# VectorE builds eight selection matrices with two wide operations in a graph network kernel

## The reference, cut to what matters

```python
h = maximum(layernorm(x), 0)
for W, root, b in three_layers:                       # indices 0, 1, 2
    out = h @ root + b
    for r in range(8):
        mask = edge_type == r
        agg = segment_sum(where(mask, (h @ W[r])[src], 0), dst)
        cnt = segment_sum(mask, dst)
        out = out + agg / maximum(cnt, 1)
    h = relu(out)
x = x + h
h = maximum(layernorm(x), 0)
a = h + segment_sum(h[src], dst)
x = x + batchnorm(relu(a @ W1 + b1) @ W2 + b2)
```

## Time and profile before

| what | us |
|---|---|
| median of three runs | 1883.6 (1880.57 to 1884.61) |
| profiled execution, whole time | 1885.77 |
| its span, first to last instruction | 1883.8 |
| TensorE, VectorE, ScalarE, GpSimd busy | 1277.2, 888.7, 645.7, 1612.1 |

### The profile page before, as it was taken

How to read it: one execution, slowest core, us unless ns; L and a number is a source line. 1 busy time by engine, 2 the same in 40 slices (tenths; PEclk the granted TensorE clock), 3 DMA queues, 4 the chain that set the end, 5 groups by cost and what they waited for, 6 DMA issues and landing times.

```text
span 1883.8 us, 18726 instructions
## 1 busy us (share of the span) xinstructions
PE 1277.2 (68%) x4614; PEld 863.5 (46%) x4614; DVE 888.7 (47%) x3270; ACT 645.7 (34%) x1146; POOL 1612.1 (86%) x2502
## 2 busy tenths in 40 slices
PE   7888665657476776666667666675566666667787
PEld 3564444434344554444444344454444444444554
DVE  5784754545442366757676666652222222122213
ACT  5404000000000376867677766732011011112123
POOL 5888888888888888888888888878888888888881
PEclk9987655555555655657565656575567675757678
DMA  7823332323232311213121312231111111111111
GB/s 240 288 81 90 102 116 71 112 72 103 80 90 62 97 46 45 90 46 90 45 90 45 91 45 79 58 96 45 46 45 45 46 45 45 46 45 46 46 46 45
DMA packets 70010, 144.25 MB, mean 77 GB/s; under 512 B 23487, under 2 KB 37048, under 8 KB 69896
## 3 DMA queue, kind: packets, MB, share of 16 engines
q0 software_dynamic: 39840, 81.67, 17.3%
q1 hardware_dynamic: 29624, 60.67, 8.9%
q10 hardware_dynamic: 432, 0.64, 0.1%
HBM read 100.23 MB, written 42.67 MB: 76 GB/s over the span
## 4 chain that ended last, share of the span: by engine, by line
POOL 75%; issue 11%; PE 9%; DMA 4%; DVE 1%; ACT 1%; another core or an unknown queue 0%; POOLq 0%; DVEq 0%; SPq 0%; ACTq 0%
POOL rows L1249 53%; POOL slow L1234 19%; DMA rows<-h_table,idx 3%; PE ps_agg L562 2%; POOL early L1239 2%; PE ps_agg L617 1%; PE ps_a L580 1%; PE ps_h L531 1%; POOL rows L1270 1%; PE ps_agg L591 1%; PE ps_a L669 0%; PE ps_a L649 0%; PE ps_a L603 0%; PE ps_h L669 0%; ACT early L733 0%
## 5 line engine op out<-in xcount | busy, mean ns | idle before, releaser
L1249 POOL DMA_INDIRECT rows<-h_table,idx x1183 | 1127.4, 953 | 199.7 <-issue 190.2
L562 PE MATMUL ps_agg<-sel,rows 128*128 128x64 f32 (+16 forms) x2780 | 734.6, 381 | 452.2 <-DMA rows<-h_table,idx 445.3
L562 PEld LDWEIGHTS ps_agg<-sel,rows 128*128 128x128 f32 x2780 | 638.7, 290 | 725.3 <-DMA rows<-h_table,idx 539.3
L964 DVE TENSOR_SCALAR sel<-iota,early,norm 128x64 f32<-128x64 f32 x1186 | 436.8, 430 | 474.4 <-PE ps_agg L562 451.9
L1234 POOL MEMSET slow<- 128x264 f32 (+1 forms) x1248 | 424.1, 340 | 0.7
L1060 DVE TENSOR_TENSOR early<-ps_a,early 128x300 f32 x416 | 197.5, 475 | 207.9 <-PE ps_a L649 160.9
L846 ACT ACTIVATE scratch<-scratch,ones 128x300 bf16<-128x300 f32 x416 | 222.6, 535 | 119.6 <-PE ps_a L649 96.6
L649 PE MATMUL ps_a<-scratch 128*128 128x300 bf16 x416 | 168.3, 405 | 113.5 <-issue 67.7
L852 ACT ACTIVATE scratch<-iota,code_lo 128x300 f32<-128x300 f32 x416 | 226.5, 545 | 12.5
L531 PE MATMUL ps_h<-w_all,xT 128*128 128x512 f32 x300 | 214.1, 831 | 6.6 <-issue 4.9
L942 DVE TENSOR_SCALAR_CACHE_REDUCE agg_s<-scratch,key_f 128x256 bf16<-128x256 int16 x416 | 194.8, 476 | 7.0 <-DMA scratch<-key_rows 5.5
(11 more groups left out here) (158 smaller groups left out, 760.5 us busy)
## 6 DMA issues: line engine op xcount, KB each, us to landing
h_table<-stage SPq DMA_DIRECT2D x65, 512.0 KB
rows<-h_table,idx POOLq DMA_INDIRECT x1183
scratch<-key_rows SPq DMA_DIRECT2D x26, 544.0 KB
h_table<-scratch SPq DMA_DIRECT2D x10, 512.0 KB
x_rows<-in_x SPq DMA_DIRECT2D x6, 256.0 KB, 6.3
w_all<-in_W SPq DMA_DIRECT2D x3, 512.0 KB, 6.6
x_table<-early SPq DMA_DIRECT2D x6, 256.0 KB, 2.3
out<-early SPq DMA_DIRECT2D x6, 256.0 KB
```

Source lines behind the costliest of these rows:

```text
L562: mm = nc.tensor.matmul(sums_of(L, k)[:, at:at + width], mine, sel[edges, G % SELS, in_window:in_window + width], start=False, stop=(t == ...
L964: done = nc.vector.tensor_scalar(mine, here, dst, weight, ALU.is_equal, ALU.mult)
L1249: pool.indirect_dma_start(rows[:, slot, :], None, table, bass.IndirectOffsetOnAxis(ap=column, axis=0)).then_inc(landed, 16)
```

## The change

`select` now handles most tiles in batches. In all of layer 0, and in layers 1 and 2 from tile 16 on, the call for the first tile of a batch compares and weighs all eight tiles at once, and the other seven calls do nothing. `select_batch` reads the eight windows of `iota` as one overlapping pattern with a step of 7 columns, compares it with the eight destinations (each repeated 64 times along its window), writes 128x512, raises the new semaphore `s_near_sel` and waits for it, and then multiplies the 128x512 in place by the eight weights, each repeated 64 times. Both are TENSOR_TENSOR, in place of eight TENSOR_SCALAR of 128x64 that compare and weigh in one pass. `s_sel` is raised by the product. The waits in front of the batch are the same, and tiles 0 to 15 of layers 1 and 2 stay as they were. That makes 47 + 50 + 50 = 147 batches.

```diff
+        s_near_sel = sem("s_near_sel")
+        batches = [0]
...
+        def select_batch(dve, L, t):
+
+            G = TILES * L + t
+            mine = sel[:, G % SELS:G % SELS + BATCH, :]
+            near = iota[:, EARLY + start_of[t]:EARLY + start_of[t] + SPAN]
+            near = bass.AP(near.tensor, near.offset, [near.ap[0], [STEP, BATCH], [1, SPAN]])
+            done = nc.vector.tensor_tensor(mine, near, dst_f[:, t:t + BATCH].unsqueeze(2).to_broadcast([P, BATCH, SPAN]),
+                                           ALU.is_equal)
+            if L < GIN:
+                done.then_inc(s_near_sel, 1)
+                batches[0] += 1
+                dve.wait_ge(s_near_sel, batches[0])
+                done = nc.vector.tensor_tensor(mine, mine, norm[:, t:t + BATCH].unsqueeze(2).to_broadcast([P, BATCH, SPAN]),
+                                               ALU.mult)
+            done.then_inc(s_sel, 1)
+
         def select(dve, L, t):
...
+            if L == 0 or t - t % BATCH >= LATE_TILES:
+                if t % BATCH == 0:
+                    select_batch(dve, L, t)
+                return
```

## The result

The changed kernel takes 1905.4 us in the median (1902.4 to 1906.7), the kernel before 1883.4: a ratio of 1.0117 with a 95% interval of 1.0101 to 1.0133. It is 22 us slower; 19 us slower was forecast.

The account below looks back on a forecast made before the run. POOL's cycle of gathers and MEMSETs was taken to bound the kernel. Collisions cost 22 us, old disturbance gives back 3, so 19 us more: 1903 us forecast, with an 8-in-10 range from 1880 to just above 1932.

Parts of the forecast that it names:

- What bounds the kernel: POOL's cycle of gather and MEMSET, 1.45 us, sets the pace: 1248 cycles make 1810 of the 1884 us.
- VectorE some 300 us less busy: Sign expected in the changed profile: VectorE's busy time falls by some 300 us.
- The length of an operation: Each of the 294 new TENSOR_TENSOR of 128x512 in the batches takes 0.69 us.
- The new wait: The product waits for the comparison, starting 0.03 us behind it; a batch holds VectorE 1.41 us; costed at nothing.
- The disputed term: VectorE operations with two SBUF inputs hold up POOL's gathers: 22 us more, between 15 and 28.
- What goes: The 1176 old TENSOR_SCALAR selections on VectorE vanish; less disturbance of POOL gains 3 us, between 0 and 8.
- the fast rival: VectorE's relief decides: POOL regains disturbance and waits, up to 18 us, about 12 likely, 1871.6 us; chance 0.12.
- No conflict: New operations do not hold up POOL's gathers; only the 3 us go, 1880.6 us; chance 0.12.
- Heavier blocking: VectorE holds from its operation's start, 48 us, 1929, or the pair blocks as one; chance 0.12 for both.
- One block of the pair: Comparison and product block POOL as one piece of 1.41 us: 79 us, 1960; within heavier blocking's chance of 0.12.
- The Trainium skill's inference: Descriptor generation on GpSimd does not conflict with two-SBUF-input VectorE operations, so the disputed term would be zero.

Follow-up runs that it names:

- its repeat: The changed kernel run again, unchanged, on a third chip, against the kernel before there: 1905.4 us, ratio 1.0119.

## Why the prediction was right

- *What bounds the kernel.* Right. POOL's busy and idle time account for the whole change (+28.6 - 7.5), and 96 us less of busy time on VectorE count nothing by themselves. The sign "VectorE some 300 us less busy" failed: 300 is the difference of the records, which overlap, and its own give 147 x 2.05 - 203 = 98 us.
- *The length of an operation.* Right: 687 and 692 ns against 0.69. Operands repeated along a window and windows that overlap cost nothing extra here.
- *The new wait.* Right: the product starts 0.04 us behind the comparison (1660.54, 1660.58), and POOL's waits for PE are 8.4 us in the profile after and 5.5 in its repeat, against 5.9 and 6.6 before. The 0.6 us of idle time that it gives PE per tile is too much (445.3 us over 1248 tiles, 0.36 each), which bears on nothing, as the term was costed at nothing.
- *The disputed term.* The mechanism is shown, by the second input taken away at equal length, by the same operation with one input in PSUM, and by the same work moved in time. The size was a little low: the gathers grew by 30 us and 25 us (30.9 and 28.0 on those that met a wide operation), 22 taken, with 28 as one end. The step that was mis-sized is where VectorE takes hold. I took the middle of 0.16 and 0.31 us; the runs put it between 0.16 (503.77: free) and 0.18 or 0.19 (1380.58: held), so the end at 0.16 was the right one, and gives 28. The formula also lets a request fall at any moment of the cycle, which does not hold for each operation: in layer 2 of the changed kernel 2 gathers asked under a comparison and 45 under a product. That the sum comes out even so fits the pair filling 1.41 of 1.45 us.
- *What goes.* Of the 3 us for old collisions, the MEMSETs gave back 1.8 (424.1 to 422.3 us), but nothing in the repeat (423.8 to 424.0), and their mean did not fall to its median (340 to 339 ns); the term was too high. The relief of VectorE, which I had left to the fast rival and costed at nothing, gave 3.5 to 7.5 us more; that VectorE's lighter load is what ends POOL's wait before layer 2 fits every profile outside the slower chip, but is argued. It is the part of that rival that came true, and it offsets the low size of the collisions: 30.2 - 1.8 - 7.5 = 21 against 22 - 3 = 19. The agreement within 3 us is thus partly luck.
- *The rivals.* No conflict: refuted by the held gathers. Heavier blocking from the operation's start: refuted for these operations by the free pairs at 0.16. One block of the pair: refuted by the halving without the product. Faster: VectorE's relief alone is worth 8 us in the kernel with one SBUF input, and did not decide.
- *The Trainium skill's inference.* "SBUF — State Buffer" of the Trainium skill infers in Who interferes with whom that issuing a DMA from GpSimd does not suffer from a VectorE operation with two SBUF inputs. For these gathers the runs disagree: 1.45 against 0.95 us with such an operation, 0.95 beside one of equal length with one input. Whether it is the writing of descriptors that waits, or the gather's reading of `idx` from SBUF, no run here tells.

## What to carry to other kernels

When GpSimd's gathers set the pace, count on VectorE not the time but the operations with two SBUF inputs, and how long each lasts: one long one stopped a gather for up to its whole length less 0.16 us, while pieces of 0.29 us cost a quarter as much in all. An input in PSUM made the same operation harmless. Before trading many short one-input operations for few long two-input ones, look in the old trace for a single pair of that kind that overlaps a gather; three such rows priced this change. An engine that gets free is worth only what the bound engine waits for it, here 3.5 to 8 us, though VectorE was busy for 96 us less.

## What the runs showed of the hardware

- A gather on POOL asks 0.13 us after its start. The outcome has an edge: asked 0.16 us into a VectorE operation with two SBUF inputs, the gather is free and VectorE takes 0.07 longer; asked 0.19 into it, the gather waits 0.51 us to the end. The edge holds where VectorE stood idle before the operation. Where it follows another operation without a gap, the edge can lie earlier: in the repeat of the kernel before, a gather that asked 0.08 us into a `close_keep` straight behind a selection took 1.56 us:

```profile
1360.91 1.56 POOL L1249 DMA_INDIRECT rows<-h_table,idx  x1 [0.17 <-issue]
1360.96 0.68 DVE L996 TENSOR_TENSOR x_rows<-x_rows,agg_s 128x512 f32<-128x512 f32 x1
```

- POOL's MEMSET, which has no input, was not held up by either operation (0.34 us at 1660.14 inside a comparison, 0.33 at 1579.42 inside a product).
- Of three chips one ran the kernel before in 1904.6 us and two in 1883.3 and 1884.2. That is as much as the change costs, so a comparison of this size holds only between kernels of one chip.
